# A four-layer vision tower: rows of a routed stage's first blocks by 0-1 products, and the third stage's first weights loaded while the LRU runs

## The reference, cut to what matters

```python
# layer 0: top 1 of 8
top1_idx = argmax(scores, -1)
for e in range(8):
    ye = silu(xn @ W1[e] + b1[e]) @ W2[e] + b2[e]
    out = where(top1_idx == e, ye, out)
return out * top1_score
...
# layers 2 and 3: top 2, with a shared expert
out = shared_expert(x)
for e in range(E):
    out = out + w[..., e:e+1] * ((silu(x @ g[e]) * (x @ u[e])) @ d[e])
```

## Time and profile before

| | us |
|---|---|
| median of 3 runs (788.59 to 790.14) | 789.73 |
| the profiled execution, its own time | 787.2 |
| its span, first to last instruction | 785.4 |
| PE busy | 683.5 (87%) |
| DVE busy | 351.6 (45%) |
| ACT busy | 255.3 (33%) |
| POOL busy | 133.1 (17%) |

### The profile page before, as it was taken

One profiled execution on the slowest core, in us unless ns is written; L12 is line 12 of the kernel. 1 busy time (PEld: TensorE's weight loads), 2 busy tenths in 40 slices (PEclk: granted clock), 3 DMA queues, 4 the chain that ended last, 5 costly groups with the idle time before them and its releaser, 6 DMA issues.

```text
span 785.4 us, 15607 instructions
## 1 busy us (share of the span) xinstructions
PE 683.5 (87%) x6255; PEld 520.7 (66%) x6303; DVE 351.6 (45%) x1035; ACT 255.3 (33%) x639; POOL 133.1 (17%) x100
## 2 busy tenths in 40 slices
PE   8998769998866798989988979999957995999996
PEld 6665558885433346765754669888945564988885
DVE  3328630005999785667668521111137742111113
ACT  1342235453633404653682312222210111222221
POOL 2000200001299700131050220000040040000004
PEclk9999879999999999999999989999987998999999
DMA  8960279925455130000003788999150555899913
GB/s 305 387 227 0 76 245 338 366 86 205 139 151 151 44 121 0 1 1 0 1 0 111 309 296 310 349 369 359 59 180 1 211 224 161 326 350 372 353 50 90
DMA packets 30931, 143.81 MB, mean 183 GB/s; under 512 B 4625, under 2 KB 16721, under 8 KB 24337
## 3 DMA queue, kind: packets, MB, share of 16 engines
q1 hardware_dynamic: 23888, 132.86, 46.4%
q0 software_dynamic: 2240, 5.90, 2.3%
q10 hardware_dynamic: 4736, 4.13, 1.6%
HBM read 133.15 MB, written 9.71 MB: 182 GB/s over the span
## 4 chain that ended last, share of the span: by engine, by line
PE 51%; DVE 19%; issue 11%; DMA 8%; POOL 7%; ACT 4%; SPq 1%; DVEq 0%; POOLq 0%; ACTq 0%
PE PS L549 48%; DVE arena L2033 5%; POOL x_slots L1502 3%; DMA x_slots<-XH,posu 2%; DMA TMP<-x_slots 2%; DMA arena<-y_slots,posu 2%; PE PS L608 2%; POOL arena L1515 2%; PE PS L572 1%; DVE stats L1596 1%; DVE stats L1589 1%; POOL arena L1541 1%; DVE arena L2158 1%; DMA y_slots<-arena 1%; DMA arena<-bc_scratch 1%
## 5 line engine op out<-in xcount | busy, mean ns | idle before, releaser
L549 PE MATMUL PS<-arena 128*64 128x64 f32 (+5 forms) x3188 | 241.5, 265 | 10.9 <-DVE arena L2161 3.1
L549 PEld LDWEIGHTS PS<-arena 128*64 128x64 f32 (+1 forms) x3188 | 202.2, 155 | 42.5 <-issue 15.4
L1819 DVE TENSOR_TENSOR arena<-arena,PS 128x384 f32<-128x384 f32 (+1 forms) x66 | 26.9, 407 | 186.6 <-ACT arena L1197 186.6
L549 PE MATMUL PS<-warm 128*128 128x512 bf16 (+2 forms) x377 | 92.6, 362 | 20.0 <-DVE rs L1580 15.3
L1515 POOL DMA_INDIRECT arena<-y_slots,posu x25 | 23.6, 944 | 321.7 <-DMA y_slots<-arena 315.0
L549 PEld LDWEIGHTS PS<-warm 128*128 128x128 bf16 (+1 forms) x425 | 38.7, 101 | 58.1 <-DVE rs L1580 18.5
L1197 ACT ACTIVATE arena<-PS 128x384 f32<-128x384 f32 (+1 forms) x66 | 27.2, 413 | 138.7 <-PE PS L549 138.7
L1528 POOL TENSOR_TENSOR arena<-arena 128x1152 f32<-128x1152 f32 x16 | 56.4, 3522 | 33.5 <-DVE arena L2033 33.5
L549 PE MATMUL PS<-arena,wsh 128*128 128x128 f32 (+3 forms) x568 | 58.0, 272 | 1.3 <-ACT arena L1189 0.7
L549 PE MATMUL PS<-arena,ident 128*128 128x512 f32 (+1 forms) x128 | 38.0, 440 | 21.5 <-POOL arena L1528 21.5
L549 PEld LDWEIGHTS PS<-arena,wsh 128*128 128x128 f32 (+1 forms) x568 | 51.7, 178 | 5.9 <-issue 2.8
(11 more groups left out here) (306 smaller groups left out, 913.7 us busy)
## 6 DMA issues: line engine op xcount, KB each, us to landing
arena<-w_moe SPq DMA_DIRECT2D x24, 2176.0 KB, 9.4
arena<-w_moe SPq DMA_DIRECT2D x9, 2052.0 KB, 9.7
wsh<-w_moe SPq DMA_DIRECT2D x8, 2176.0 KB, 10.6
arena<-bc_scratch SPq DMA_DIRECT2D x32, 288.0 KB, 3.8
wsh<-w_moe SPq DMA_DIRECT2D x3, 2052.0 KB, 11.2
y_slots<-arena ACTq DMA_DIRECT2D x19, 128.0 KB, 9.3
wx<-w_moe SPq DMA_DIRECT2D x1, 2176.0 KB, 18.4
wx<-w_sh SPq DMA_DIRECT2D x1, 2176.0 KB, 8.9
```

The source lines that it names most:

```text
L549: return nc.tensor.matmul(out_, l, r, start=start, stop=stop, skip_group_check=True)
L1819: ins = v.tensor_tensor(firsts(hid_b[x][:, 0:full], n_), firsts(sg_s[x][:, 0:full], n_), firsts(PS[:, 2 * x + 1, 0:full], n_), ALU.mult)
```

## The change

It has four parts. In stages two and three the first two blocks take their rows by 0-1 products, and in stage one the third block does too. Two such matrices share one buffer (`b // 2` and a column offset), all use PSUM banks 7 and 6 in turn, and VectorE builds them between products of the shared expert. `load_rows` sends the large rows ahead of the small ones. Stage three's ring is turned, so that its first two blocks use buffers 2 and 3; their weights are then loaded straight behind the shared expert's, before the LRU instead of behind it; and these loads and the shared expert's stand behind a new wait for the last gather of stage two (`row14`). On VectorE, `row_weights` of stage two moves behind the last product of the shared expert, and `gate_shares` and `row_weights` of stage three move in between them.

```diff
-RING = {"ffn0": (3, 0, 1, 2), "ffn2": (0, 1, 2, 3), "ffn3": (0, 1, 2, 3)}
+RING = {"ffn0": (3, 0, 1, 2), "ffn2": (0, 1, 2, 3), "ffn3": (2, 3, 0, 1)}
-ONE_HOT = ("ffn0",)
+ONE_HOT = {"ffn0": 3, "ffn2": 2, "ffn3": 2}
+HOT0 = {"ffn0": 0, "ffn2": 5, "ffn3": 7}
+HOT_PLACED = {"ffn0": 4, "ffn2": 5}
...
@@ SP, load_rows
-                    for i, (u0, u1) in enumerate(((0, 6), (6, n_s))):
-                        sp.dma_start(x_small[i][:, 0:u1 - u0, :], x_slots[mid + HB * u0:mid + HB * u1, :]
-                                     .rearrange("(u r) d -> r u d", r=HB)).then_inc(sem("x0"), 16)
+                    def small():
+                        for i, (u0, u1) in enumerate(((0, 6), (6, n_s))):
+                            sp.dma_start(x_small[i][:, 0:u1 - u0, :], x_slots[mid + HB * u0:mid + HB * u1, :]
+                                         .rearrange("(u r) d -> r u d", r=HB)).then_inc(sem("x0"), 16)
+
                     sp.dma_start(x_big[:, 0:NP[name], :], x_slots[0:mid, :].rearrange("(u r) d -> r u d", r=SB))\
                         .then_inc(sem("x1"), 16)
                     for b in range(sent, nb):
                         sp.dma_start(rows_of(name, b), x_slots[slot_of(name, b):slot_of(name, b) + SB, :]).then_inc(sem("x1"), 16)
+                    small()
...
@@ SP, between stages two and three
             sp.wait_ge(sem("downd"), 2 * BLK0["ffn3"])
+            sp.wait_ge(sem(f"row1{NT - 1}"), 16)
             load(wx0[:, :], w_sh3, "sh3")
-            sp.wait_ge(sem("tm_ready"), 8 * NT)
             begin, run = expert_blocks("ffn3", w_moe3)
             begin()
+            sp.wait_ge(sem("tm_ready"), 8 * NT)
             run()
...
@@ PE, x_chosen
-                    pe.wait_ge(sem("one_hot"), 2 * ONE_HOT.index(name) + b + 1)
+                    pe.wait_ge(sem("one_hot"), HOT0[name] + b + 1)
+                    at_ = HB * (b % 2)
-                                last = mm(PS[64 * c:64 * (c + 1), 7 - b, SB * d:SB * d + HB],
+                                last = mm(PS[64 * c:64 * (c + 1), 7 - b % 2, SB * d:SB * d + HB],
                                           tile(XH, j)[:, 128 * d + 64 * c:128 * d + 64 * (c + 1)],
-                                          one_hot[b][0:TILE_N[j], j, 0:HB], j == 0, j == NT - 1)
+                                          one_hot[b // 2][0:TILE_N[j], j, at_:at_ + HB], j == 0, j == NT - 1)
@@ PE, emit
-                    if not before and name in ONE_HOT:
-                        x_chosen(1)
+                    if b + 1 < ONE_HOT[name]:
+                        x_chosen(b + 1)
                     elif after:
                         x_transposes(b + 1, 1 - p, after)
@@ PE, routed
-                if name in ONE_HOT:
-                    x_chosen(0)
-                else:
-                    x_transposes(0, 0, "S")
+                x_chosen(0)
...
@@ DVE, places
                 v.tensor_copy(posu[:, 0:nk, :], pos[:, 0:nk, :]).then_inc(sem("pos_ready"), 1)
+                if name == "ffn0":
+                    chosen_rows(name, 1)
...
-                if name in ONE_HOT:
-                    for b in range(name == "ffn0", 2):
-                        chosen_rows(name, b)
+                if name == "ffn0":
+                    chosen_rows(name, 2)
@@ DVE, stage two
                 if c == 2:
                     placed_rows("ffn2", 0)
-                if c == 4:
-                    row_weights("ffn2", True)
+                elif c < 5:
+                    chosen_rows("ffn2", c - 3)
+            row_weights("ffn2", True)
             side_tiles(6 * NT, 2)
@@ DVE, stage three
-            shared("ffn3", CH2, (0,), first=2)
+            for c in range(2, CH2):
+                shared_product("ffn3", CH2, c)
+                if c < 4:
+                    chosen_rows("ffn3", c - 2)
+                elif c == 4:
+                    gate_shares("ffn3", True, False)
+                    row_weights("ffn3", True)
             side_tiles(8 * NT, 3, range(0, 3))
-            gate_shares("ffn3", True, False)
-            row_weights("ffn3", True)
```

More of the change, by code:

```diff
@@ L701, in between @@
                         place_transposes(name, nb - 1, 1)
-                if name in ONE_HOT:
-                    x_chosen(0)
-                else:
-                    x_transposes(0, 0, "S")
-                over_blocks(name, emit, between if name in ONE_HOT else None)
+                x_chosen(0)
+                over_blocks(name, emit, between if name == "ffn0" else None)
                 down(nb - 1, (nb - 1) % 2, 1, "P")
@@ L714, in place_transposes @@
                 i = b - NBLK[name]
-                n = PLACED0[name] + b - (NBLK[name] - LASTS[name]) + 1
-                pe.wait_ge(sem("one_hot"), n + 2)
+                pe.wait_ge(sem("one_hot"), HOT_PLACED[name])
                 for j in range(NT):
@@ L1662, in placed_rows @@
                 dve.wait_ge(sem("comb_ready"), COMBS[name])
-                if name in ONE_HOT:
-                    dve.wait_ge(sem("xt_t"), BLK0[name] + 2)
+                if name == "ffn0":
+                    dve.wait_ge(sem("xt_t"), BLK0[name] + ONE_HOT[name])
                 for j in range(NT):
@@ L1688, in chosen_rows @@
             def chosen_rows(name, b):
-                if b == 0:
-                    dve.wait_ge(sem("xt_t"), BLK0[name]) if BLK0[name] else None
+                at_ = HB * (b % 2)
                 for j in range(NT):
-                    ins = v.tensor_scalar(one_hot[b][0:TILE_N[j], j, 0:HB], tri[0:TILE_N[j], 4, 0:HB], cnt[0:TILE_N[j], b, j:j + 1],
+                    ins = v.tensor_scalar(one_hot[b // 2][0:TILE_N[j], j, at_:at_ + HB], tri[0:TILE_N[j], 4, 0:HB], cnt[0:TILE_N[j], b, j:j + 1],
                                           mks[0:TILE_N[j], b, j:j + 1], ALU.is_equal, ALU.mult)
@@ L1698, in chosen_rows @@
                         ins.then_inc(sem("one_hot"), 1)
-                dve.wait_ge(sem("one_hot"), 2 * ONE_HOT.index(name) + b + 1)
+                dve.wait_ge(sem("one_hot"), HOT0[name] + b + 1)
             def places(name, second, between=None):
```

## The result

The changed kernel takes 779.45 us (median of 4 runs, 776.23 to 780.43), the one before took 789.93 on the same chip: ratio 0.986, 95% interval 0.984 to 0.988. The forecast was 776.6, with a range of 773.0 to 782.0.

What follows compares the result with a forecast made beforehand. Bound: the rows' way through HBM at three stage starts, and one collision of transfers. Gains 4.1 + 2.2 + 4.9 + 1.9 = 13.1 us took the profiled 787.2 to 774.1; with 2.5 for the median, 776.6, range 773.0 to 782.0.

Steps and rivals of the forecast that it cites:

- Stage one, 4.1 forecast: Stage one: large rows there at 109.7, so block 3's first product starts at 114.6 instead of 118.64; gain 4.1 us.
- the scatter's slip: Stage one: its last scatter ends later by the full 1.2 us that block 3's weights come later; nothing the other end.
- Stage two, 2.2 forecast: Start of stage two: block 2's transposes come at 469.5 instead of 471.7; gain 2.2 us.
- so 7.9: Stage two, block 0 to block 2's transposes: 7.57 us, less 1.2 for the clock, plus 1.5 for block 1's rows.
- Stage three, 4.9 forecast: Start of stage three: block 2's transposes come at 662.2 instead of 667.1; gain 4.9 us.
- 7.03 - 1.2 + 1.5: Stage three, block 0 to block 2's transposes: 7.03 us now, less clock loss, plus block 1's rows; 7.3 us.
- The gather, 1.9 forecast: Gather behind stage two: with the shared expert's load behind it, adds end at 586.0 instead of 587.9; gain 1.9 us.
- The turns: Rival, gather: late for its own ten transfers, sharing takes turns; minus 1.9, plus 1.2, 777.3 us; chance 0.15.
- The large rows become the new wait: Rival, all three stages: large rows land 3 us slower than forecast, gains 8.7 in all, 781.0 us; chance 0.10.
- Stage one gives it back: Rival, late stage one: the start's 4.1 us end in a wait for the last weights, 780.7 us; chance 0.08.
- no gaps worth the name: Inside a routed stage PE has no such gaps, so whatever shortens a load there gives nothing.
- Slower: Rival: the changed kernel is slower through the clock, shown by clock 0.50 in the starts; chance 0.03.

Runs made afterwards that it cites:

- e1: Kernel before with only the new wait: stage three's shared expert's weights load behind stage two's last gather; 787.44 us, ratio 0.9975.
- e7: Changed kernel with stage one as before (two blocks by 0-1 products, small rows first); 782.50 us, ratio 0.992.
- e3: Changed kernel with all 0-1 products 128 columns wide, 10 instead of 20 per block; 776.03 us, ratio 0.985.
- e8: As e6, with 0-1 products 128 columns wide in stage one alone; 776.71 us, ratio 0.984.
- e11: As e8, with block 0's 0-1 products of stages two and three ahead of the transposes of the shared expert's result; 772.45 us, ratio 0.978.
- e2: Changed kernel with the small rows loaded ahead of the large ones again; 780.77 us, ratio 0.989.
- e5: Changed kernel with stage three's ring as before and its first weights loaded behind the LRU, new wait kept; 780.12 us, ratio 0.988.
- e12: As e11, with ScalarE's copy of block 0's rows in stage two ahead of its placement matrix copies; 769.10 us, ratio 0.978.
- a0: Changed kernel run once more without any edit; 780.69 us, ratio 0.988.
- e4: Changed kernel with 64 more small products in PE's idle time behind stage two; 782.62 us, ratio 0.992.
- e10: As e11, with 0-1 products of stages two and three 128 columns wide too; 773.98 us, ratio 0.980.
- e6: Changed kernel without the 8 constant products ahead of stage two, the placement matrix wait moved to the stage's end; 777.64 us, ratio 0.985.

## Why the prediction was right, and where it was not

The total was right by 2.9 us: forecast 776.6, measured 779.45. All four gains have the place and the sign that I gave them. That is shown by the waits that are gone in the profile, by e1 for the gather and by e7 for stage one; the 0-1 products of stages two and three were never taken out alone.

- **Stage one, 4.1 forecast, 4.75 measured.** The wait for the large rows moved in at 109.4 as said. Two sizes in it were off and cancelled: the scatter's slip (1.2 taken, 2.3 measured) and the landing behind it (4.6 taken, 3.4 measured). Block 3's weights are issued 1.2 us later, as said (94.75 us). By the gate's products the scatter lands 0.8 us later than before with wide products (e3, e8, e11), whose weights are as late, and 2.0 to 2.3 with narrow ones: some 1.3 us go with the narrow products. That their instruction pages compete with the scatter is my reading of it; it wasn't tried alone, and a rival stands beside it: block 0's result is also written to HBM 2.4 us sooner with narrow products than with wide ones (issued 19.8 us behind the gate in the changed kernel, 22.2 in e3). With both parts undone (e7) the stage is at 96.1 us again. The order alone (e2) is worth 3 us in the arrival of the rows; how much of it reaches the stage's end no run secures. And the 4.75 is the best of the five profiles with this code: their middle one, 93.0 us, is a gain of 3.2. There is luck in how near it came to the forecast.
- **Stage two, 2.2 forecast, 1.35 measured.** The step that failed is "so 7.9" from block 0 to block 2's transposes: it was 8.8. I had taken 1.5 us for block 1's products from their duration alone. Of the work, those 40 pairs cost that; as instructions they are a third of 128 pairs, by the theory a third of a page, and the next page wasn't there (1.32 us). Without the stop it would be 7.5: the clock gave back 0.4 more than my 1.2 (2.83 less 1.62, at clocks of 0.50 and 1.00), since the 112 instructions behind the first 48 had run partly at the low clock too (before: 4.47 us, 0.51 from 467.0 to 468.2 us; e3: 4.10).
- **Stage three, 4.9 forecast, 3.45 measured.** The same step and term: "7.03 - 1.2 + 1.5", 1.21 us of stop.
- **The gather, 1.9 forecast, 1.8 measured**, and 2.0 alone (e1).
- **Costs taken at nothing.** VectorE's moved steps cost nothing that shows. The weights during the LRU gave nothing, as said (e5).
- **The rivals.** "The turns", by which the gather and the load would share the DMA engines in turns and the gather would be late for its own ten transfers: out (e1). With the load out of its way the kernel was 2.0 us faster, so no sharing shielded it here. "The large rows become the new wait": not in stages two and three of the changed kernel, but in stage three of e12, by 1.09 us. "Stage one gives it back": not; a stop late in the stage is 1.48 us in one profile and 2.81 with a low clock behind it in the other (a0). In the first it costs next to nothing, because the kernel before has a wait there that is gone:

```profile
164.95 2.03 PE L549 MATMUL PS<-arena 128*64 128x64 f32 x48 [1.29 <-ACT arena L1189]
```

Block 3 starts 4.83 us sooner and 4.75 reach the end of the stage. My "no gaps worth the name" had passed over those 1.29 us.
- **"Slower".** This rival was a low clock through the starts of the stages. The clock was 1.00 through those of stages two and three (454 to 466 and 645.0 to 656.5 us), with all their half-width products. A low one would have cost 0.65 to 0.75 us more for each of work: 3.00 us against 1.82 and 2.83 against 1.62. Where the clock did fall in a stage and PE had not waited for 2 us or more just before, a stop of over 2 us mostly stood ahead (a0, e4, e11), but not always (stage one of e10: 0.50 from 92 to 100 us), and one such stop left it at 1.00 (e8); so what takes it down isn't shown.

What the trace of before could have told: the number of instructions that a start adds. It showed the durations of the products, and a count of 40 beside each; only the durations went into the sum.

**Still open:** what makes the packet of instructions start 0.3 us behind a boundary in one run and 4.9 in another, and with it why stops of one kind last from 0.2 to 2.8 us; the 2 us between stages one and two that some profiles have; and the 2.1 us in the LRU's stretch of e6.

## What to carry to other kernels

Small matmuls cost twice in this kernel: 40 pairs took 1.82 us, and with 40 fewer of them in stage one the stop of stage two stood 38 pairs further on (e7). Ahead of each of its 38 stops PE had taken 4.8 to 6.2 us for 128 pairs, with the DMA engines busy for 0.68 to 1.19 of that time (DMA share of the windows). Where a profile looks like that and shows such stops, count pairs from stop to stop (here the places repeated every 128); try fewer and wider products where something else covers their length (here stage one: 3.5 us shorter in the profile of e3 than in the changed kernel's, 4.1 in e8's than in e6's, though the medians don't secure it); and look for the stop in a later stage once products are added or removed (e4: 63 pairs sooner and 1.1 us longer). And look for the large load that has been issued just ahead of a small gather that is on the path: one wait on SP was worth 2 us (0.6 to 3.3).

## What the runs showed of the hardware

- TensorE stopped for 0.2 to 2.8 us where the trace shows nothing that it waits for, in stages two and three at places that repeat every 128 pairs of matmul and weight load: 64 more products moved one 63 pairs sooner (e4), 8 and 40 fewer moved one 8 and 38 later (e6, e7), 60 fewer 60 later (e8), and the one of stage three from 245 to 178 (e6, e8; 245 + 60 - 128 = 177). It went on 2.2 to 2.9 us behind the start of a 16384-byte instruction packet on queue 8, in 38 stops of 14 profiles.
- A group of 20 half-width products (128*64 weights, 64 columns; 40 in the profile) took 1.82 us, 10 of full width took 2.76 to 2.86 (e3): half their number was dearer by 1.0 us, and no stop of over 0.4 us stood in stages two and three (e3, e10).
- Behind stops of 2.03, 2.28, 2.35 and 2.81 us the granted clock was down to 0.59 (e4, 158 to 160 us), 0.52 (e11, 468 to 470), 0.50 (e4, 658 to 660) and 0.50 (a0, 161 to 165). Behind those of 1.2 to 1.9 us in stages two and three and late in stage one it was 1.00. After 2.30 us in e8 it stayed at 1.00 too (649.5 to 662 us), so length alone didn't decide.
